# One store and its fetches moved behind the eviction of k's transposes, and a table load with them

## The reference, cut to what matters

```python
for i in range(DEPTH):                               # DEPTH = 6
    x = attn_layer(shift_tokens(x), Wqkv[i], q_scale[i], k_scale[i], Wo[i]) + x
    x = ffn_layer(shift_tokens(x), ln_g[i], ln_b[i], W1[i], b1[i], W2[i], b2[i]) + x
# attn_layer: qkv = x @ Wqkv; q, k = l2norm * scale, rotary tables;
#   sim = q k^T * 8 over two windows of 32 keys, softmax, times v, then @ Wo
# ffn_layer: layernorm, xn @ W1 + b1 = a, gate; (a * gelu(gate)) @ W2 + b2
```

## Time and profile before

| | us |
|---|---|
| median of 3 runs | 3716.09 (3702.31 to 3723.45) |
| the profiled execution's own time | 3709.85 |
| its span, first to last instruction | 3708.1 |
| the stretch of the layers, 760 to 3640 | 2880, 48 steps of 60.0 |

### The profile page before, as it was taken

The page is one execution under the profiler, slowest core; times in us unless marked ns, Lnnn a source line. Parts: engine busy times, 40 slices in busy tenths (PEclk is TensorE's granted clock), DMA queues, the critical chain, the costliest instruction groups (busy, mean ns, idle before and its releaser), DMA issues.

```text
span 3708.1 us, 161688 instructions
## 1 busy us (share of the span) xinstructions
PE 3540.4 (95%) x70540; PEld 2685.4 (72%) x70540; DVE 3182.2 (86%) x4422; ACT 2863.6 (77%) x5288; POOL 2575.7 (69%) x2106
## 2 busy tenths in 40 slices
PE   6999999869999999999999999999999999999996
PEld 2222222358888888888888888888888888888885
DVE  7999999578888888888888888888888888888883
ACT  3999999757777777877777777878777777777773
POOL 3222111278878888888888888888888888878883
PEclk8999999889999999999999999999999999999998
DMA  4110000034444444444544444444444444444442
GB/s 121 40 41 23 23 20 18 15 91 117 120 112 109 120 121 120 111 112 111 137 109 117 112 109 130 115 118 109 113 117 125 113 117 110 130 116 119 114 116 60
DMA packets 210250, 366.48 MB, mean 99 GB/s; under 512 B 37106, under 2 KB 81734, under 8 KB 209222
## 3 DMA queue, kind: packets, MB, share of 16 engines
q1 hardware_dynamic: 209482, 355.05, 35.9%
HBM read 236.73 MB, written 111.67 MB: 94 GB/s over the span
## 4 chain that ended last, share of the span: by engine, by line
PE 55%; ACT 8%; DVE 7%; issue 4%; POOL 4%; DMA 0%; ACTq 0%; POOLq 0%; SPq 0%; DVEq 0%
PE PA L1366 11%; PE PB L1442 9%; PE PD L1394 7%; PE PD L1455 7%; PE PB L1366 5%; PE PC L1416 4%; PE PC L1470 4%; PE PC L1494 3%; PE PA L1425 3%; POOL T L1278 2%; ACT L1653 1%; DVE ss L1757 1%; DVE T L1751 1%; PE PD L1358 1%; ACT G L1651 1%
## 5 line engine op out<-in xcount | busy, mean ns | idle before, releaser
L1260 POOL TENSOR_TENSOR T<-T 128x1024 f32<-128x1024 f32 x384 | 907.0, 2379 | 8.7 <-DVE T L1751 8.6
L1278 POOL TENSOR_TENSOR T<-T,rn 128x1024 f32<-128x1024 f32 x384 | 731.4, 1905 | 27.6 <-POOL rn L1271 1.3
L1366 PE MATMUL PA<-Wqkv,XS 128*128 128x512 f32 x2304 | 632.4, 410 | 13.4 <-DVE XS L1705 9.1
L759 DVE TENSOR_REDUCE negmax<-p_max 128x1 f32<-128x1024 f32 x512 | 589.0, 1215 | 15.6 <-PE p_max L659 13.5
L821 ACT ACTIVATE E<-p_low 128x512 f32<-128x512 f32 x1024 | 554.0, 596 | 28.0 <-PE p_low L683 17.3
L1366 PEld LDWEIGHTS PA<-Wqkv,XS 128*128 128x128 f32 x2304 | 417.1, 194 | 93.9 <-issue 11.3
L1394 PE MATMUL PD<-ident,T 128*128 128x128 f32 x3072 | 414.5, 278 | 30.4 <-ACT qT L1613 17.6
L1723 DVE TENSOR_REDUCE sm<-Ew 128x16 f32<-128x1024 f32 x192 | 233.5, 1216 | 241.7 <-ACT Ew L1584 241.7
L1757 DVE TENSOR_REDUCE ss<-SQ 128x32 f32<-128x2048 f32 x192 | 436.8, 2275 | 0.0
L1442 PE MATMUL PB<-ET,VW 64*64 64x32 f32 x24576 | 398.8, 220 | 7.2 <-issue 6.2
L1442 PEld LDWEIGHTS PB<-ET,VW 64*64 64x64 f32 x24576 | 377.1, 135 | 38.0 <-issue 30.8
(11 more groups left out here) (167 smaller groups left out, 6989.1 us busy)
## 6 DMA issues: line engine op xcount, KB each, us to landing
VW<-v_rows SPq DMA_DIRECT2D x768, 256.0 KB, 5.1
v_rows<-Vs SPq DMA_DIRECT2D x192, 512.0 KB, 3.4
Wraw<-in_Wqkv SPq DMA_DIRECT2D x40, 192.0 KB, 4.4
QA<-parts_q SPq DMA_DIRECT2D x384, 16.0 KB
KA<-parts_k SPq DMA_DIRECT2D x192, 32.0 KB
fs<-XC SPq DMA_DIRECT2D x48, 127.0 KB
parts_q<-AO SPq DMA_DIRECT2D x8, 384.0 KB, 2.6
parts_k<-AO SPq DMA_DIRECT2D x8, 384.0 KB, 3.3
```

The lines of the kernel that those rows point to most:

```text
L759: dve.tensor_reduce(negmax[:, qh, c, qt:qt + 1], p_max[:, k % 2, :], axis=AX.X, op=ALU.max, negate=True).then_inc(s_mr.sem, 1)
L1260: pool.tensor_tensor(out=t_, in0=t_, in1=T2[:, i * HALF:(i + 1) * HALF], op=ALU.add).then_inc(ad.sem, 1)
L1278: pool.tensor_tensor(out=t_, in0=t_, in1=rn[:, p, i * LH:(i + 1) * LH].unsqueeze(2).broadcast_to([P, LH, LD]), op=ALU.mult).then_inc(no.se ...
L1366: mm = pe.matmul(pair[:, half, :], XS[:, b, i, 1:P + 1], Wqkv[:, l % 2, j, lo:lo + 512], start=(k == 0), stop=(k == 2))
```

## The change

The store of tile s-1 no longer waits for the scores of s-2 but for the third eviction of tile s-1's transposes, kT; the fetches of s-2 follow it at once as before. The load of the table with log and exp, which stood right behind the last gelu in slot 2 (ahead of the halo of k and all evictions of transposes), now stands behind kT and kH and ahead of the input's eviction. TensorE's, VectorE's and GpSimd's programs are the same.

```diff
@@ on_sp
-            if is_tile(s - 2):
-                sp.wait_ge(sc.sem, sc.at(s - 2))
             if is_tile(s - 1):
+                sp.wait_ge(te.sem, te.at(s - 1, 3))
                 values_out(s - 1)
             if is_tile(s - 2):
                 values_in(s - 2)
@@ on_act, ff_gate
             act.activation(G[0:c, i, :], src, ACT.Gelu, bias=b1[0:c, 1, i:i + 1]).then_inc(gd.sem, 1)
-            if i == NCH - 1:
-                act.preload_act_table_set(LOG_EXP)
@@ on_act, slots
             if is_tile(s - 1):
                 transpose_k(s - 1)
+            if d == 2 and is_step(u - 2):
+                act.preload_act_table_set(LOG_EXP)
             if is_tile(s + 1):
                 input_T(s + 1)
```

## The result

The changed kernel takes 3738.71 us in the median of 7 runs (3731.76 to 3752.44), the kernel before 3715.72 (3702.31 to 3723.45, 7 runs). The ratio is 1.0073, 95% interval 1.0053 to 1.0094: slower, by 0.5 to 0.9%. The profiled execution took 3737.51 us, its span 3735.7, against 3709.85 and 3708.1 before. Behind L1208 the lines of the changed kernel have a number one lower (L1559 evicts v, L1415 are the scores, L1454 is the output); the table load that moved is L1677.

A forecast was written before the change was run, and what follows sets the result against it. The prediction took TensorE to set the time. Its terms, 29 - 14 - 16 + 24 = +23 us on the profiled 3709.85, gave 3733, or 3739 on the median's scale, written as 3738; range 3695 to 3780.

The forecast's parts named there:

- C: Ends of slots: blocks asked for during attend find free rings, taking away stalls; -16 us, bounds 0 and -33.
- B: Slot 2: moving the table load gains 0.3 us a step; -14 us, bounds 0 and -31.
- A: Slot 0 into slot 1: v's eviction waits for the later store, 0.6 us a step; +29 us, bounds 0 and +43.
- D: Scores of the next slot: blocks asked for at the branch come late behind full rings; +24 us, bounds 0 and +65.
- priced at nothing: Slots 1, 2 and 3: the later store was taken to cost nothing there.
- PE stands 32.7 us: Ahead of L1455 at slot ends: unexplained idle time of 32.7 us in 94 pieces, taken for late instructions.
- 1: Rival: the store's wait finds slack and instruction fetches don't get worse; -30, 3686 us, chance 0.15.
- 2: Rival: gains and losses cancel, the block at the branch being asked for early enough; -1, 3715 us, chance 0.28.
- 5: Rival: instruction blocks play no part and the 32.7 us are something else; +15, 3731 us, chance 0.05.
- 3: Rival: instructions are late in nearly every slot, D at its upper bound; +64, 3780 us, chance 0.12.
- 4: Rival: the table load only changes its place in ScalarE's full row in slot 2; +37, 3753 us, chance 0.05.

The follow-up runs named there:

- e4_split: The change, but the store stays behind the scores and only the four fetches wait for kT; table load moved as in the change: ratio 0.9939.
- e7_late_fetch: The kernel before with only the four fetches held back until kT; store and table load as before: ratio 0.9945.
- e11_thin_again: The change with small fetches (32 of 512 columns from tile 8 on), a repeat in more rounds: ratio 1.0029.
- e10_both: The change with two buffers Vs (half of the rotary tables kept) and small fetches (32 of 512 columns from tile 8 on): ratio 0.992.
- e2_store: The kernel before with only store and fetches moved; the table load stays ahead of q's evictions: ratio 1.0101.
- e1_load: The kernel before with only the table load moved; store and fetches stay where they were: ratio 0.9994.
- e9_place: The change with slot 1's first projection instruction laid at place 41 of a block of 256 instead of 105: ratio 1.0104.
- e3_vs2: The change with two buffers Vs, so v's eviction waits for the store of two tiles before; half of the rotary tables kept: ratio 1.0008.
- e8_late_store: The kernel before with only the store waiting for kT, placed behind the fetches, which stay at the scores: ratio 1.0751.

## Why the prediction was right

The forecast was 3738 against 3738.71 measured, and the four parts of the sum are the four that the runs found. By the runs the sum is C -20, B -5 (e4_split less e7_late_fetch in the 40 steps, times 1.2), A and D together +50: +25, and the profiled executions differ by 27.7. Point by point:

**A**, +29 predicted. Right in mechanism, place and size of the shift: in e11_thin_again v's eviction in slot 0 is at 11.96 and in e10_both at 11.36, the 0.6 of the prediction, and slots 2 and 3 are as long with the wait as without (15.29 and 15.27, 16.21 and 16.20), as "priced at nothing" said. Slot 1 grew by 0.69 (14.58 to 15.27), so A is 33 to 35 us by the profiled executions, and 40 by the timings. v's eviction waits in slot 0 in 35 of 40 steps, where "nearly all" was said. It waits as often in slot 1 (38 of 40), where the prediction saw only a pause being used up; there, too, the wait costs nothing that shows in slot 2. The landing in slot 3 fell from 6.7 to 3.4, as taken. The prediction did not see that the store now stands in a loop; it read one passage of it, slot 0 to 1, and that was enough here, since the loop of 14.8 is just below the mean slot.

**B**, -14 predicted; -5 in the 40 steps (e4_split less e7_late_fetch; by timings 2, with intervals of 0.0015 to 0.002), 1 to 10 by the other pair (e2_store and the change), 0 alone. So B is small, and its size is not settled. The working holds in its own slot. Timeline of after:

```profile
1996.20 1.04 PE L1424 MATMUL PA<-ident,Ew 128*128 128x128 f32 x8
...
1997.07 1.04 PE L1393 MATMUL PD<-ident,T 128*128 128x128 f32 x8
...
1999.46 1.28 ACT L1677 ACT_TABLE_LOAD   x1
...
2001.08 0.57 ACT L1553 ACTIVATE XS<-PD 64x128 fp32r<-64x128 f32 x2
...
2002.22 1.02 ACT L1597 ACTIVATE OT<-PB 128x1024 f32<-128x1024 f32 x1
...
2003.36 0.74 PEld L1454 LDWEIGHTS PD<-Wo,OT 128*128 128x128 f32 x6 [0.38 <-issue]
```

k's transposes are 0.87 behind those of the exponentials (0.9 predicted, 1.42 in the earlier trace rows), the input's eviction is 11.08 into the slot (11.11 before), OT 12.22 (12.25), and the output's weight loads start 0.12 behind OT's end and its matmuls 0.15, 0.25 earlier in the slot than in the earlier trace rows. The gain of 0.3 ends at OT, as said. What was mis-sized is what lies behind: with B slot 2 is 0.22 shorter and slot 3 0.10 longer (e7_late_fetch to e4_split: 15.47 to 15.25, 16.12 to 16.22), so nearly half is given back. Where the fetches are early (e1_load), slot 0 takes it all back.

**C**, -16 predicted, -20 measured in e7_late_fetch: right in cause, as the third packet of the slot shows. The size is partly luck. It was taken as half of a row of idle time, and the gain is hardly in that row: of 16.4 us in 40 steps 16.1 are busy time. The sign was badly chosen, too. "The idle time ahead of L1455 falls below 16" did not happen; it is 32.1 us in 91 pieces after. e7_late_fetch shows C's fall, to 18.1 in 53, and so does e2_store, the change without B (18.0 in 53); e4_split, which adds B to e7_late_fetch, has 35.4 in 91. The 38 more pieces are B's own: the weight loads wait ahead of the output in most steps, like the [0.38] above. Two parts of the change wrote to one row. Most of the row is idle time of the weight load, too (27.4 of it before), so "PE stands 32.7 us" said more than the row does.

**D**, +24 predicted, +22 (40 steps) to +26 (timings) alone, and on top of A +15 by the 40 steps (2418.88 less 2406.26, times 1.2), 7 to 16 by the timings. Right in cause, as e9_place shows. The prediction expected it in slots 1 to 3; it came in slot 1 alone. Why can be worked out from medians over 41 steps. A block's first instruction runs 2.69 behind its packet's start, where it is waited for (slot 1; 2.66 in e3_vs2 and 2.65 in e9_place). I take the same for the other slots, as an estimate. In the change the packets start 0.46, 1.85, 1.16 and 1.39 us into slots 0 to 3, so the block is there at 3.15, 4.54, 3.85 and 4.08; the 55th score was at 3.75, 3.70, 4.39 and 4.39 in the kernel before. Only slot 1 is late, by 0.84, and the measured gap is 0.82. That 24 came so near to 22 is luck: it was chosen between 0 and 65 from a row of another place (27.4 of whose 32.7 us are idle time of the weight load), and the slots were not told apart.

**The sum.** A and D overlap in slot 1, which the prediction ignored. B came out 9 smaller than said, C 4 larger, A some 6 larger, D 2 smaller, and the overlap takes 7: 23 + 9 - 4 + 6 - 2 - 7 = 25. The errors nearly cancel, so that forecast and measurement lie within 1 us is luck; the signs and causes of A, C and D are not.

**Rivals.** 1 and 2 (D at nothing) and 5 (blocks play no part) are refuted by e9_place and e3_vs2; 3 (D at its upper bound) by the three slots in which the block still comes in time; 4 (the load gives nothing) is nearly what happened to B, but not to the total. That crossings between blocks are mostly hidden, as the Trainium skill, page "Runtime: NRT & Kernel Launch", section "Instruction fetch mechanics", has it, holds in three slots of four here for the block asked for at the branch, and fails in slot 1 of the change, where the packet starts 1.85 us into the slot behind the store and its fetches (1.5 MB): 38.7 us in 51 pieces. The rule of the Trainium skill, page "DMA: Bandwidth & Descriptors", section "Rules for kernel authors", to issue early and wait late, holds for the store (A) and not for the fetches: the same fetches issued some 4 us later gained 20 us (e7_late_fetch), since nobody waited for them and instructions did.

**A better version.** e4_split and e7_late_fetch separate the two DMAs that the change moved together: the store early, the fetches behind kT. e4_split moves the table load too. At 0.9939 (0.9918 to 0.9959) and 0.9945 (0.9931 to 0.996) they beat before by 0.6% and the change by 1.3%; between the two nothing can be told.

## What to carry to other kernels

Two DMAs that stand next to each other on a queue have different slack: before moving them together, ask of each who waits for it, and whether its landing closes a loop from tile to tile, since in a loop that sets the time every microsecond of landing is paid again in each turn. Instructions of an unrolled program are a DMA client like any other: put large transfers where no block is asked for that is needed soon, and find out with a shifted block placement whether an unexplained stall is one. When a change has several parts, choose for each a sign in a row that no other part writes to.

## What the runs showed of the hardware that I had not expected

- In front of slot 1 the packet of an instruction block starts 1.06 us behind the branch that asks for it in the kernel before, when the rings are quiet. In the change, where the store and its four fetches began to be issued 3.4 us before the branch (1969.92 to 1973.3), it starts 3.38 us behind. Where it is waited for, the first instruction of the block runs 2.7 us behind the packet's start, though the packet itself takes 1.3 (medians over 41 steps).
- In slots 0 to 2 a store of 512 KB lands in 3.2 to 3.6 us with no fetches issued ahead of it (means over 40 steps, all kernels but e9_place, which has 3.8 in slot 1), and in 3.8 to 4.2 behind four fetches of 256 KB (e8_late_store). In slot 3 it lands in 6.3 to 7.4 right behind the shift of rows, in 3.3 to 3.5 some 4 us later, and in 7.6 behind the shift and four fetches.
- The load of a table takes 1.28 us, and where its operands are ready the activation behind it starts 0.01 later (in slot 2 of the change: 1990.40 + 1.28, then 1991.69).
